# Moving the norms of batches 2 and 3, batch 2's query split and one load in the two preludes of a four-block transformer kernel

## The reference, cut to what matters

```
x = x + cross_attention(layernorm(x), ctx, tau, delta, weights L0)   # 120 keys, 16 heads of 16
x = x + ffn(layernorm(x), ...)     # self attention of 16 heads, then a mixture of 8 experts, top 1
x = x + cross_attention(layernorm(x), ctx, tau, delta, weights L1)
x = x + set_ffn(layernorm(x), ...) # 32 experts x 4 sets, chosen by a maximum within 32 tokens
```

## Time and profile before

| | us |
|---|---|
| median of 3 runs | 876.43 |
| lowest, highest | 871.1, 876.84 |
| the profiled execution's own time | 876.62 |
| its span | 874.5 |

### The profile page before, as it was taken

One profiled execution on the slowest core, in us unless ns is written; L12 is line 12 of the kernel. 1 busy time (PEld: TensorE's weight loads), 2 busy tenths in 40 slices (PEclk: granted clock), 3 DMA queues, 4 the chain that ended last, 5 costly groups with the idle time before them and its releaser, 6 DMA issues.

```text
span 874.5 us, 16791 instructions
## 1 busy us (share of the span) xinstructions
PE 741.9 (85%) x6289; PEld 567.6 (65%) x6289; DVE 475.4 (54%) x1207; ACT 364.6 (42%) x672; POOL 233.1 (27%) x313
## 2 busy tenths in 40 slices
PE   7657988879978988787999999988587887788898
PEld 6544656656656655456889899987464565456775
DVE  3346677876788778543122122223356677654575
ACT  2244655555566545610323222212244546544323
POOL 1323243333433221222111111007223434332000
PEclk9788999999999999989999999999788999976999
DMA  7749556974544664534837476504456353061202
GB/s 167 138 70 181 90 93 87 116 101 72 86 83 71 87 94 151 194 122 150 319 131 225 135 245 176 175 22 101 53 89 110 56 85 51 27 260 51 98 14 85
DMA packets 59853, 102.01 MB, mean 117 GB/s; under 512 B 7220, under 2 KB 49908, under 8 KB 54742
## 3 DMA queue, kind: packets, MB, share of 16 engines
q1 hardware_dynamic: 57341, 95.45, 48.0%
q0 software_dynamic: 1872, 5.11, 2.9%
q10 hardware_dynamic: 560, 0.38, 0.1%
HBM read 55.38 MB, written 7.21 MB: 72 GB/s over the span
## 4 chain that ended last, share of the span: by engine, by line
PE 59%; DVE 15%; ACT 7%; issue 6%; POOL 5%; DMA 5%; SPq 2%; ACTq 0%; DVEq 0%; POOLq 0%
PE U L905 9%; PE PS L894 8%; PE MB L722 8%; PE MB L821 6%; PE U L797 4%; PE MB L740 4%; DVE nma L1274 4%; PE MB L756 4%; PE MB L977 3%; PE PS L779 3%; PE MB L987 2%; DMA x<-in_x 2%; PE PS L1011 1%; DVE st L1226 1%; DVE nmb L1274 1%
## 5 line engine op out<-in xcount | busy, mean ns | idle before, releaser
L1274 DVE TENSOR_REDUCE nma<-MB 128x2 f32<-128x512 f32 (+1 forms) x192 | 122.4, 671 | 43.2 <-PE MB L756 43.2
L1099 ACT ACTIVATE Pa<-PS 128x1024 f32<-128x1024 f32 (+1 forms) x96 | 97.7, 1025 | 49.3 <-PE PS L779 48.0
L756 PE MATMUL MB<-QKa 99*128 99x120 bf16 (+1 forms) x512 | 71.5, 254 | 23.2 <-DMA QKa<-dsx 4.6
L905 PE MATMUL U<-mw,mdT 128*128 x368 | 83.6, 380 | 4.5 <-DVE mdT L1446 2.3
L894 PE MATMUL PS<-mzT,mw 128*128 128x128 f32 x736 | 86.3, 276 | 1.3 <-ACT mzT L1121 0.8
L894 PEld LDWEIGHTS PS<-mzT,mw 128*128 128x128 f32 x736 | 84.1, 192 | 2.2 <-DMA mw<-in_mw 1.2
L1454 DVE TENSOR_TENSOR yt<-U,mb 128x256 f32<-128x256 f32 x23 | 9.8, 424 | 127.6 <-PE U L905 127.6
L905 PEld LDWEIGHTS U<-mw,mdT 128*128 128x128 f32 x368 | 68.2, 190 | 13.8 <-issue 5.5
L756 PEld LDWEIGHTS MB<-QKa 99*128 99x128 bf16 x512 | 39.5, 102 | 53.4 <-issue 15.7
L1537 POOL TENSOR_TENSOR mv<-mv,vec 128x2 f32<-128x2 f32 (+1 forms) x40 | 30.6, 765 | 121.1 <-DVE mv L1231 69.8
L779 PE MATMUL PS<-QKa 101*128 101x256 bf16 (+1 forms) x384 | 59.6, 280 | 0.4 <-DMA QKa<-mTa 0.4
(11 more groups left out here) (209 smaller groups left out, 1385.9 us busy)
## 6 DMA issues: line engine op xcount, KB each, us to landing
mw<-in_mw SPq DMA_DIRECT2D x31, 1024.0 KB, 6.0
QKa<-spa SPq DMA_DIRECT2D x144, 128.0 KB, 4.7
Qb<-spb SPq DMA_DIRECT2D x48, 128.0 KB, 4.6
Oa<-Uba SPq DMA_DIRECT2D x16, 256.0 KB, 2.5
v<-in_v SPq DMA_DIRECT2D x1, 4096.0 KB, 13.6
v<-in_v SPq DMA_DIRECT2D x4, 1024.0 KB, 12.1
yb<-yt SPq DMA_DIRECT2D x23, 128.0 KB, 1.7
QKa<-spa SPq DMA_DIRECT2D x24, 120.0 KB, 4.6
```

Source lines behind the costliest of these rows:

```text
L756: i = e.matmul(b[:, keys * j:keys * j + keys], Q[0:99, h0 + j, 128 * qt:128 * qt + 128], K[0:99, h0 + j, 0:keys], start=True, stop=True)
L905: i = e.matmul(U[:, 0:256], mdT[j % 2][:, f, :], w2[:, bass.ds(expert[j], 1), f, :], start=f == 0, stop=f == 7)
L1099: e.activation(p[0:keys, :], ps[0:keys, :], ACT.Exp, scale=0.25).then_inc(sems["exp"], 1)
L1274: e.tensor_reduce(A.nm[qt][:, h0:h0 + heads], b[:, 0:heads * keys].rearrange("p (h s) -> p h s", h=heads), AX.X, ALU.max, negate=True).the ...
```

## The change

It moves steps in the list, changes how many idle matmuls follow some steps, and issues one load earlier:

```diff
-T_CROSS_2 = ((-2.9, -2.6, -0.96, -0.96, -0.8, -0.6), (), (-2.75, -2.45, -0.96, -0.96, -0.8, -0.6))
+T_CROSS_2 = ((-2.45, -2.3, -0.96, -0.96, 0.03, 0.1), (), (-2.75, -2.45, -0.96, -0.96, 0.03, 0.1))
+T_CROSS_3 = (-1.2, -1.1, 0.05, 0.25, 0.5, 0.75)
...
-T_SUM = {1: -3.57, 2: -3.8}
+T_SUM = {1: -3.57, 2: -3.8, 3: -4.23}
...
-            task(T_CROSS_2[L] if near and m == 2 else at(T_CROSS), [("na", n, 0)], [("nb", n, 0)], [("zt", n)],
+            task(T_CROSS_2[L] if m == 2 else T_CROSS_3 if m == 3 else at(T_CROSS), [("na", n, 0)], [("nb", n, 0)], [("zt", n)],
...
-IDLE = {("in", 0): 20, ("zt", 0): 9, ("zt", 1): 8, ("kp", 2): 48,
+IDLE = {("in", 0): 20, ("zt", 0): 9, ("zt", 1): 8, ("kp", 2): 34,
...
-        ("se", NTILE - 1): 90, ("zt", 16): 5, ("zt", 17): 16, ("qp", 17): 40}
-IDLE.update({("mx", n, u): 2 for n in (0, 16) for u in range(7)})
+        ("se", NTILE - 1): 90, ("zt", 16): 5, ("zt", 17): 16, ("qp", 17): 54}
+IDLE.update({("mx", n, u): 3 + 5 * (u == 7) for n in (0, 16) for u in range(8)})
...
             e.dma_start(A.dr, D["delta"]).then_inc(sems["d_delta"], 16)
+            load_x(2)
             e.dma_start(A.Qt[96:99, :, :], ones[0:3, :].rearrange("p (s n) -> p s n", s=4)).then_inc(sems["d_ones_a"], 16)
...
             e.dma_start(ctx[:, :, CK2:], D["ctx"][:, :, CK2:]).then_inc(sems["d_ctx"], 16)
-            load_x(2)
```

## The result

| | before | after |
|---|---|---|
| median of 20 executions | 876.63 us | 865.56 us |
| lowest, highest | 869.9, 885.94 | 860.38, 872.37 |
| span of the profiled execution | 874.5 us | 861.1 us |

The change makes the kernel 1.1% faster: ratio 0.9887, 95% interval 0.9859 to 0.9915. The forecast was 858.2, a gain of 18; 11 were measured. The ratio leaves out executions more than 1.5% above the fastest, which are more often the kernel's before, so the difference of the plain medians, 11.1, is a little more than the ratio's 9.9.

The account below looks back on a forecast made before the run. PE, busy 85%, was taken as the bound, so only its idle and low-clock time could be won. Gains of 13.0 and 7.1 us in the two preludes, 20.1, less one clock fall, gave 18.2: 858.2 us, range 853 to 866.

Parts of the forecast that it names:

- A: First prelude up to the first maxima: POOL takes batch 0's queries earlier, maxima start at 26.5, gain 4.2 us.
- B: First maxima to `mt 0` or `mt 16`, at the high clock: gain 0.8 us in the first prelude, 0.1 in the second.
- C: `mt 0` or `mt 16` to the first scores' end, at the high clock: gain 2.0 us first prelude, 1.0 second.
- D: PE's idle hole between first scores and `zt 3` or `zt 19` closes: gain 5.7 us first prelude, 5.8 second.
- E: `zt 3` to the end of `qp 3`, `zt 19` to that of `qp 19`: gain 0.3 us first prelude, 0.2 second.
- bank wait: Behind `zt 3`, `mx 1 1` waits for ACT to copy its bank out: copy ends 40.3, PE there at 39.0.
- The cover of part A: `kp 2` and 34 idle matmuls leave PE free at 24.7 to 26.3, before the maxima at 26.5; margin 0.2 us at worst.
- rival 1: Idle matmuls in the maxima run at the low clock: 865 us if in one prelude, 872 in both; chance 0.12.
- One fall of 1.9: One clock fall hitting a query projection, 1.9 us, taken off the summed gain for both preludes together.
- Rival 2: Batch 2's query split lands too late for `mx 2 0`, some 3 us in each prelude: 864 us; chance 0.12.

Follow-up runs that it names:

- c2: Changed kernel with the context's second load cut in two and batch 2's and 18's query split behind the turned tile's copy: median 858.03 us, ratio 0.9772 to before.
- c3: c2 with 58 idle matmuls behind `kp 2` instead of 34: median 863.01 us, ratio 0.9837 to the kernel before.

## Why the prediction was wrong

The differences of starts on PE's timelines, in us; before: the first trace, the repeated one and the kernel with the other prelude changed; after: the changed kernel, the repeated one and the one with the load put back.

| stretch | three with the old order | three with the new | gain of the means | forecast |
|---|---|---|---|---|
| first `kp 0` to first maxima (A) | 23.7, 23.9, 23.6 | 21.6, 22.2, 20.8 | 2.2 | 4.2 |
| to `mt 0` (B) | 6.8, 7.5, 7.3 | 6.0, 8.1, 7.9 | -0.1 | 0.8 |
| to the first scores (C) | 5.6, 4.7, 5.0 | 6.7, 3.4, 3.4 | 0.6 | 2.0 |
| scores to `zt 3` (D, the scores in it) | 7.0, 7.0, 6.9 | 0.5, 0.4, 0.4 | 6.5 | 5.7 |
| `zt 3` to the first `pv` of batch 1 (E and on) | 29.4, 30.7, 30.5 | 28.9, 31.4, 31.3 | -0.3 | 0.3 |
| second: `zt 16` to `mx 16 0` | 15.7, 16.6, 15.1 | 17.5, 17.1, 15.2 | -0.8 | 0 |
| to `mt 16` (B) | 6.1, 5.9, 5.9 | 5.9, 5.9, 5.9 | 0.1 | 0.1 |
| to the scores (C) | 4.5, 4.9, 5.6 | 3.4, 3.4, 3.4 | 1.6 | 1.0 |
| scores to `zt 19` (D) | 6.9, 6.9, 6.9 | 0.4, 0.4, 0.4 | 6.5 | 5.8 |
| `zt 19` to the first `pv` of batch 17 (E and on) | 28.7, 28.2, 28.8 | 29.1, 29.1, 30.5 | -1.0 | 0.2 |

The new order of the first prelude also stands in the kernel with that prelude alone, which isn't in the table: 22.7, 6.0, 8.1, 0.5 and 28.7. With it the gains are 1.9, 0.2, -0.3, 6.5 and 0.1. The kernel with the second prelude alone has 15.6, 5.9, 3.4, 0.4 and 32.3 in its lower rows, which makes the last of them -1.7. And the kernel with only the norms of batches 3 and 19 moved, whose steps up to the first maxima stand as before, took 22.1 for the first row: A's gain may be as small as 1.5.

**Right**: part D in both preludes, the larger part of the gain; the wait of DVE at `nb` behind POOL's split was the cause, as read from the earlier trace rows. B and C of the second prelude. The bank wait of part E was foreseen, at its place and in kind.

**Part A failed in its sum.** I followed SP's issues and took the delta rows to go out at 21.85. `kr 0` also waits for `dsx`, which the code says and which I didn't price; before, it landed 1.8 ahead of its use, hidden by the wait that goes. The delta rows went out at 24.73 and landed at 27.6. Shown by SP's 5.4 us and by the kernel with the load put back. The gain is 2.2. The moved load seems to make it worse, by 1.2 us on the mean: where it stands ahead of the whole context (six traces), the context landed at 19.0 to 20.3 and `dsx` at 24.3 to 25.8; where it stands behind (five), at 17.2 to 18.9 and at 23.0 to 24.6. The cover of part A failed too: the 3.64 us of waiting for the context let the clock fall, so `kp 2` and the 34 idle matmuls took 2.46 and 5.02 instead of 1.8 and 3.8, and PE was free at 27.60, not at 24.7 to 26.3. In this trace that is the very time at which the delta rows landed.

**Part B and E of the first prelude failed by the clock.** I took the high clock for the maxima. With A's wait for the delta rows back in its place, PE idled 3.4 to 4.6 us ahead of them in two of the three traces with the new order, and the idle matmuls ran at half speed: rival 1, to which I gave 0.12, is what happened there, though the clock came back on the way: 8 us, not 10. It takes back what B should give. In the third trace the wait for the context took the place of this idle time and the maxima rows came late instead. So C came out at its best bound where the maxima ran slowly (3.4), and its bound by the landing was too low where they ran fast: 6.0 to landing. The landings say when: in the nine of the fourteen traces in which the maxima rows were issued at most 1.6 us before the last of batch 1's query parts had landed, they took 2.07; in the five where it was 3.2 us or more, 4.3 to 9.0. With the context whole, fast maxima thus run into batch 1's parts and win little. (The 2.0 us that part C quotes from the Trainium skill ("DMA: Bandwidth & Descriptors", section on the anatomy of one DMA) is a fit for transfers issued from GpSimd; these went out from SP.)

**Part E of the second** lost 1.0 where 0.2 was to be gained: the wait was 2.0 and the clock fell behind it. The 0.8 lost ahead of the second maxima, where 14 more idle matmuls were to cost nothing, isn't explained; the traces of the old order spread over 1.5 us there, those of the new over 2.3.

The marks sum up to 8.8 in the first prelude (13.0 forecast; 8.4 with the fourth kernel) and 6.4 up to `pv 17 0` in the second (7.1; 5.9 with the fourth). That is 15.2; from `pv 17 0` to the sort 0.5 is lost again (means of 109.2 and 109.7), which leaves 14.7 where 10 to 12 were measured (9.9 and 11.0 by the two ratios, 11.1 and 12.0 by the medians). Part of the rest is in a stage that the change doesn't touch. The last expert tile waits 2.33 us in every kernel. Timelines of PE, the first of the kernel before and the second of the changed one:

```profile
584.82 3.72 PE L905 MATMUL U<-mw,mdT 128*128 x16 [2.33 <-DVE mdT L1446]
```

```profile
569.99 5.40 PE L906 MATMUL U<-mw,mdT 128*128 x16 [2.33 <-DVE mdT L1447]
```

Windows of the same stretches (PE, PEld, DVE, ACT, POOL busy; clock), again before and after:

```profile
583.00:589.00 6.00, 4.18 (x22) 3.62 (x23) 1.51 (x6) 0.00 (x0) 0.00 (x0) 1.00 0.07 25
```

```profile
570.00:576.00 6.00, 6.00 (x24) 4.92 (x25) 0.39 (x1) 0.00 (x0) 0.00 (x0) 0.72 0.01 3
```

The same idle time let the clock fall in the one and not in the other. From the first to the last expert matmul it is 176.8 us in one case and about 180 in the other; the kernel with only the second prelude changed, whose first 580 us are the kernel before, has 180.3, so the change doesn't cause it. The sort has 31.6 or 35.6 in the same way, the repeated kernel before 35.6. With such steps a pair of traces differs by several us of luck: the two first traces differ by 13.4, of which 6.6 come from a stage without any change: from batch 1's first `pv` to the first expert matmul it is 331.9 before and 325.3 after; of the twelve other traces one has 324.9 and the rest have 331.6 to 333.4. What stays open is where the missing 3 to 5 us go, and whether the shifted kernels fall into the slower case more often (about 180 in seven of the eleven traces whose first prelude is changed, in one of three with the old one); fourteen traces don't tell.

**Range and sum.** The step that failed first is the issue of the delta rows, put at 21.85 and measured at 24.73; the low clock in B follows from that wait, and the late maxima rows in C and the bank wait in E come on top. One fall of 1.9 for both preludes was too little. My range ended at 866.0; the median was just inside, the ratio's 0.9887 of the median shown before, 866.5, just outside. Rival 2 didn't show in the changed kernel: `mx 2 0` wasn't released by a DMA. It comes near, though: in c2 and c3, which have the split later still, PE waits 0.9 and 1.6 us for batch 2's query parts.

## What to carry to other kernels

When a wait goes, list every semaphore that the released step waits for, with the landing of each, and not only the one that the profile names: the next one may be a small transfer that was hidden by a microsecond or two. Idle matmuls held the clock where the wait behind them was short (0.85 us in c3), but they double in length when it has fallen (here 0.11 and 0.21 us), so the wait must be closed first. And order steps on the copying engine by who needs the result first: a query split ahead of the copy that frees a bank cost a wait of 2 us and a fall of the clock; with the split behind the copy the wait was 0.94.

## What the runs showed of the hardware

Three transfers of 1.9 KB landed 9.3 to 11.4 us after their issues (13.30 to 15.41, landed 24.7) when 720 KB of context had been issued ahead of them. Over eleven traces with the 720 KB they landed at 23.0 to 25.8, over three with 240 KB at 21.8 to 23.4, whether the first was issued at 13.3 to 13.9 or at 15.0 to 15.9.

A 16 KB transfer from SP's queue landed 2.07 us after its issue in nine traces, in all of which the last of six 128 KB parts issued ahead of it landed at most 1.6 us after that issue; it took 4.3 to 7.4 where the parts landed 3.2 us or more after it, and then landed 1.1 to 1.6 behind them. From ACT's queue, with twelve parts ahead, it took 9.0. ACT was held 1.24 us for that one issue; SP takes 0.67 for it.

2.33 us of idle time in the same place let TensorE's clock fall in 8 of 14 traces and not in the other 6: 5.40 against 3.72 us for the 16 matmuls behind it.
